# Gate and up of a routed feed-forward layer from operands split into two rounded parts, high and low parts of the rows side by side

## The reference

```python
C = max(1, math.ceil(T * K * CAP_FACTOR / E))        # 592 * 2 * 1.25 / 8 = 185 rows per expert
xb = buf[:E * C].reshape(E, C, D)                    # normalised rows, 8 x 185 x 256
gu = jnp.einsum('ecd,efd->ecf', xb, w12)             # 2048 columns: gate and up
g, u = jnp.split(gu, 2, axis=-1)
h = jax.nn.silu(g) * u
yb = jnp.einsum('ecf,edf->ecd', h, w3)
```

## Time and profile before

| | us |
|---|---|
| median of 3 runs | 254.06 |
| lowest, highest | 251.88, 254.31 |
| the profiled execution, its own time | 253.29 |
| its span, first to last instruction | 251.3 |
| mean granted TensorE clock | 0.892 of full |
| TensorE busy, matmuls | 206.7 (82%) |
| VectorE busy | 88.1 (35%) |
| ScalarE busy | 76.7 (31%) |
| POOL busy | 55.6 (22%) |

### The profile page before, as it was taken

How to read it: one execution, slowest core, us unless ns; L and a number is a source line. 1 busy time by engine, 2 the same in 40 slices (tenths; PEclk the granted TensorE clock), 3 DMA queues, 4 the chain that set the end, 5 groups by cost and what they waited for, 6 DMA issues and landing times.

```text
span 251.3 us, 3542 instructions
## 1 busy us (share of the span) xinstructions
PE 206.7 (82%) x1297; PEld 187.9 (75%) x1297; DVE 88.1 (35%) x277; ACT 76.7 (31%) x226; POOL 55.6 (22%) x55
## 2 busy tenths in 40 slices
PE   0185957989997774089999999999999999999970
PEld 0175947964765543079999999999999999999960
DVE  6849874444578745002211111111211112111110
ACT  2433311734544213011722222232222223322230
POOL 0445343000014445200002104003040040220404
PEclk9999995995589755558999999999999999999997
DMA  7935995510002122268109239077191480400101
GB/s 244 339 109 131 334 340 223 214 81 1 0 27 69 61 62 84 67 169 305 81 5 394 106 124 388 6 292 241 26 430 54 188 329 3 167 9 3 22 9 16
DMA packets 10299, 36.15 MB, mean 144 GB/s; under 512 B 3328, under 2 KB 6738, under 8 KB 7978
## 3 DMA queue, kind: packets, MB, share of 16 engines
q1 hardware_dynamic: 7514, 31.90, 35.0%
q0 software_dynamic: 2336, 2.13, 4.3%
q10 hardware_dynamic: 432, 1.90, 2.1%
HBM read 31.42 MB, written 5.35 MB: 146 GB/s over the span
## 4 chain that ended last, share of the span: by engine, by line
PE 71%; DVE 8%; DMA 7%; issue 5%; POOL 4%; ACT 2%; POOLq 1%; SPq 1%
PE bank L536 34%; PE bank L548 16%; DMA x_flat<-in 5%; PE bank L520 3%; DVE hn L765 2%; PE bank L467 2%; POOL token_rows L991 2%; PE bank L422 2%; PE bank L559 1%; POOL rstd L978 1%; PE bank L435 1%; PE bank L386 1%; PE bank L447 1%; PE bank L388 1%; PE bank L387 1%
## 5 line engine op out<-in xcount | busy, mean ns | idle before, releaser
L536 PE MATMUL bank<-xb,w 128*128 128x185 f32 x512 | 94.4, 329 | 1.1 <-ACT xb L687 1.1
L536 PEld LDWEIGHTS bank<-xb,w 128*128 128x128 f32 x512 | 84.8, 196 | 1.7 <-issue 1.2
L949 DVE TENSOR_TENSOR hid<-bank,sg 128x185 f32<-128x185 f32 x64 | 22.5, 351 | 116.8 <-ACT sg L699 116.8
L1008 POOL DMA_INDIRECT out<-yw,slot_token x16 | 23.8, 1489 | 122.1 <-ACT yw L719 119.7
L548 PE MATMUL bank<-hid,w 128*128 128x185 f32 x256 | 50.2, 320 | 0.0
L699 ACT ACTIVATE sg<-bank 128x185 f32<-128x185 f32 x64 | 20.9, 326 | 92.1 <-PE bank L536 92.1
L548 PEld LDWEIGHTS bank<-hid,w 128*128 128x128 f32 x256 | 42.1, 189 | 0.0
L335 PE MATMUL bank<-wp_hi,x_hi 128*111 128x256 f32 x36 | 11.2, 310 | 12.7 <-DVE x_lo L771 12.7
L335 PEld LDWEIGHTS bank<-wp_hi,x_hi 128*111 128x111 f32 x36 | 7.0, 194 | 12.9 <-issue 12.9
L991 POOL DMA_INDIRECT token_rows<-rowbuf,dest x12 | 11.6, 968 | 13.4 <-DVE dest L908 11.6
L520 PE MATMUL bank<-ident,rows_in 128*128 128x128 f32 (+1 forms) x32 | 7.9, 300 | 7.1 <-DMA rows_in<-token_rows 7.1
(11 more groups left out here) (137 smaller groups left out, 254.3 us busy)
## 6 DMA issues: line engine op xcount, KB each, us to landing
w<-in SPq DMA_DIRECT2D x8, 2048.0 KB, 10.7
w<-in SPq DMA_DIRECT2D x8, 1024.0 KB, 4.8
x_flat<-in SPq DMA_DIRECT2D x6, 333.0 KB, 10.8
token_rows<-rows_in SPq DMA_DIRECT2D x1, 1728.0 KB
rows_in<-token_rows SPq DMA_DIRECT2D x8, 144.0 KB
w_sb<-in ACTq DMA_DIRECT2D x1, 1024.0 KB, 9.0
wp_sb<-in ACTq DMA_DIRECT2D x1, 768.0 KB, 5.7
out<-h SPq DMA_DIRECT2D x5, 111.0 KB
```

What stands on the lines that cost most here:

```text
L536: mm = pe.matmul(o, w[:, part, k, :], xb[b][:, k, :], start=(k == 0), stop=(k == KD - 1))
L949: dve.tensor_tensor(hid[:, step % 4, :], bank[GU_BANK[step % len(GU_BANK)]][:, NS:2 * NS], sg[:, step % 2, :], ALU.mult).then_inc(hid_done, 1)
L1008: pool.indirect_dma_start(out=out, out_offset=bass.IndirectOffsetOnAxis(ap=slot_token[0:n, e, s:s + 1], axis=0), in_=yw[b][s][0:n, :], in_ ...
```

## The change

`gate_up` no longer multiplies float32 operands. The rows of an expert are first scaled to float32 (`xf`), then VectorE's new `split_tokens` copies them as fp32r (the high part) and subtracts that for the low part; both lie side by side in `xb`, 186 columns each (`NP`, 185 made even). The weights of each step go through a ring of 4 places (`w_ring`): ScalarE's `weight_hi` rounds 512 columns, VectorE's `weight_lo` subtracts. For each of 4 pairs of part and half TensorE now does a wide matmul, the high weights with all 372 columns, and a narrow one, the low weights with the 186 high columns, added to the first 186 columns of the result. Gate and up take one bank each, and two pairs of banks are used in turn. ScalarE copies the second halves of both banks out (`take_lo`), VectorE adds them to the first halves (`total`), and `silu` and `hidden` read the sum from SBUF. `gate_up` waits for `sum_done` of the step two earlier. SP waits for `w12_lo_done` where it waited for `gate_up_in_psum`, and `xf` is one buffer where `xb` was two and still is.

```diff
+NP = NS + NS % 2
+RING = 4
...
-        bank = [ctx.enter_context(nc.psum_tensor(f"bank{i}", [P, 512], F32)) for i in range(8)]
+        psum = ctx.enter_context(nc.psum_tensor("psum", [P, 8, 512], F32))
+        bank = [psum[:, i, :] for i in range(8)]
...
-        xb = [sb(f"xb{b}", [P, KD, NS]) for b in range(2)]
+        xf = sb("xf", [P, KD, NS])
+        xb = [sb(f"xb{b}", [P, KD, 2, NP], F32R) for b in range(2)]
+        w_ring = sb("w_ring", [P, RING, 2, PIECE], F32R)
         sg = sb("sg", [P, 2, NS])
+        gu = sb("gu", [P, 2, 2, NP])
+        gu_lo = sb("gu_lo", [P, 2, 2, NP])
         hid = sb("hid", [P, 4, NS])
...
                 if e >= 3:
-                    sp.wait_ge(gate_up_in_psum, FC * (e - 2))
+                    sp.wait_ge(w12_lo_done, FC * (e - 2))
                 sp.dma_start(w12[e % 3][:, :], w12T[e]).then_inc(w12_in[e % 3], 16)
...
-            GU_BANK, YT_BANK, XB_BANK, Y_BANK = (0, 1, 2, 7), (3, 4), 5, 6
+            GU_BANK, YT_BANK, XB_BANK, Y_BANK = ((0, 1), (2, 3)), (4, 7), 5, 6
...
                 pe.wait_ge(rows_back[e], 48)
                 if e >= 1:
-                    pe.wait_ge(xb_done, KD * e)
+                    pe.wait_ge(xf_done, KD * e)
...
             def gate_up(e, fc):
 
                 step, b = FC * e + fc, e % 2
+                pe.wait_ge(w12_lo_done, step + 1)
                 if fc == 0:
-                    pe.wait_ge(w12_in[e % 3], 16 * (e // 3) + 16)
-                    pe.wait_ge(xb_done, KD * (e + 1))
-                if step >= len(GU_BANK):
-                    pe.wait_ge(hid_done, step - len(GU_BANK) + 1)
-                w = w12[e % 3][:, fc * PIECE:(fc + 1) * PIECE].rearrange("p (n k f) -> p n k f", n=2, k=KD)
+                    pe.wait_ge(xb_done, e + 1)
+                if step >= 2:
+                    pe.wait_ge(sum_done, step - 1)
+                hi, lo = (w_ring[:, step % RING, n, :].rearrange("p (n k f) -> p n k f", n=2, k=KD) for n in range(2))
                 for part in range(2):
-                    o = bank[GU_BANK[step % len(GU_BANK)]][:, part * NS:(part + 1) * NS]
+                    o = bank[GU_BANK[step % 2][part]][:, 0:2 * NP]
                     for k in range(KD):
-                        mm = pe.matmul(o, w[:, part, k, :], xb[b][:, k, :], start=(k == 0), stop=(k == KD - 1))
+                        mm = pe.matmul(o, hi[:, part, k, :], xb[b][:, k, :, :].rearrange("p a c -> p (a c)"), start=(k == 0), stop=False,
+                                       skip_group_check=True)
+                        mm = pe.matmul(o[:, 0:NP], lo[:, part, k, :], xb[b][:, k, 0, :], start=False, stop=(k == KD - 1),
+                                       skip_group_check=True)
                 mm.then_inc(gate_up_in_psum, 1)
...
             def take_tokens(e):
                 act.wait_ge(xT_in_psum, e + 1)
+                if e >= 1:
+                    act.wait_ge(xb_done, e)
                 for k in range(KD):
-                    act.activation(xb[e % 2][:, k, :], bank[XB_BANK][:, k * D:k * D + NS], ACT.Identity,
-                                   scale=gamma_t[:, k:k + 1], bias=beta_t[:, k:k + 1]).then_inc(xb_done, 1)
+                    act.activation(xf[:, k, :], bank[XB_BANK][:, k * D:k * D + NS], ACT.Identity,
+                                   scale=gamma_t[:, k:k + 1], bias=beta_t[:, k:k + 1]).then_inc(xf_done, 1)
+
+            def take_lo(e, fc):
+                step = FC * e + fc
+                act.wait_ge(gate_up_in_psum, step + 1)
+                if step >= 2:
+                    act.wait_ge(sum_done, step - 1)
+                act.activation(gu_lo[:, step % 2, :, :], psum[:, 2 * (step % 2):2 * (step % 2) + 2, NP:2 * NP],
+                               ACT.Copy).then_inc(gu_lo_done, 1)
+
+            def weight_hi(step):
+                if step % FC == 0:
+                    act.wait_ge(w12_in[step // FC % 3], 16 * (step // FC // 3) + 16)
+                if step >= RING:
+                    act.wait_ge(gate_up_in_psum, step - RING + 1)
+                act.activation(w_ring[:, step % RING, 0, :], w12[step // FC % 3][:, step % FC * PIECE:(step % FC + 1) * PIECE],
+                               ACT.Copy).then_inc(w12_hi_done, 1)
 
...
             def silu(e, fc):
                 step = FC * e + fc
-                act.wait_ge(gate_up_in_psum, step + 1)
+                act.wait_ge(sum_done, step + 1)
                 if step >= 2:
                     act.wait_ge(hid_done, step - 1)
-                act.activation(sg[:, step % 2, :], bank[GU_BANK[step % len(GU_BANK)]][:, 0:NS], ACT.Silu).then_inc(silu_done, 1)
+                act.activation(sg[:, step % 2, :], gu[:, step % 2, 0, 0:NS], ACT.Silu).then_inc(silu_done, 1)
...
+            for step in range(RING - 1):
+                weight_hi(step)
             take_tokens(0)
             for e in range(EXPERTS):
                 for fc in range(FC):
+                    take_lo(e, fc)
+                    if FC * e + fc + RING - 1 < STEPS:
+                        weight_hi(FC * e + fc + RING - 1)
                     silu(e, fc)
...
-                dve.tensor_tensor(hid[:, step % 4, :], bank[GU_BANK[step % len(GU_BANK)]][:, NS:2 * NS], sg[:, step % 2, :],
+                dve.tensor_tensor(hid[:, step % 4, :], gu[:, step % 2, 1, 0:NS], sg[:, step % 2, :],
                                   ALU.mult).then_inc(hid_done, 1)
 
+            def weight_lo(step):
+                dve.wait_ge(w12_hi_done, step + 1)
+                dve.tensor_tensor(w_ring[:, step % RING, 1, :], w12[step // FC % 3][:, step % FC * PIECE:(step % FC + 1) * PIECE],
+                                  w_ring[:, step % RING, 0, :].bitcast(F32), ALU.subtract).then_inc(w12_lo_done, 1)
+
+            def total(e, fc):
+                step = FC * e + fc
+                dve.wait_ge(gu_lo_done, step + 1)
+                both = psum[:, 2 * (step % 2):2 * (step % 2) + 2, :]
+                dve.tensor_tensor(gu[:, step % 2, :, :], both[:, :, 0:NP], gu_lo[:, step % 2, :, :], ALU.add).then_inc(sum_done, 1)
+
+            def split_tokens(e):
+                dve.wait_ge(xf_done, KD * (e + 1))
+                if e >= 2:
+                    dve.wait_ge(gate_up_in_psum, FC * (e - 1))
+                dve.tensor_copy(xb[e % 2][:, :, 0, 0:NS], xf[:, :, :]).then_inc(xb_hi_done, 1)
+                dve.wait_ge(xb_hi_done, e + 1)
+                dve.tensor_tensor(xb[e % 2][:, :, 1, 0:NS], xf[:, :, :], xb[e % 2][:, :, 0, 0:NS].bitcast(F32),
+                                  ALU.subtract).then_inc(xb_done, 1)
+
+            for b in range(2):
+                dve.memset(xb[b][:, :, :, NS:NP].bitcast(F32), 0.0)
+            for step in range(RING - 1):
+                weight_lo(step)
+            split_tokens(0)
             for e in range(EXPERTS):
                 for fc in range(FC):
+                    total(e, fc)
+                    if FC * e + fc + RING - 1 < STEPS:
+                        weight_lo(FC * e + fc + RING - 1)
                     hidden(e, fc)
+                    if e + 1 < EXPERTS and fc == 6:
+                        split_tokens(e + 1)
```

More of the change, by code:

```diff
@@ L241, in vit_tower @@
         slots_done = sem("slots_done")
+        xf_done = sem("xf_done")
+        xb_hi_done = sem("xb_hi_done")
+        w12_hi_done = sem("w12_hi_done")
+        gu_lo_done = sem("gu_lo_done")
+        sum_done = sem("sum_done")
+        w12_lo_done = sem("w12_lo_done")
         gate_up_in_psum = sem("gate_up_in_psum")
```

4 lines of the change are left out of this document (2 added, 2 removed).

## The result

| | before | changed |
|---|---|---|
| median of the runs, us | 254.19 (4 runs) | 263.28 (4 runs) |
| lowest, highest | 251.88, 254.48 | 262.38, 265.43 |
| ratio, 95% interval | | 1.039 (1.030 to 1.049) |
| profiled execution, its span | 253.29, 251.3 | 264.17, 262.2 |
| mean granted clock | 0.892 | 0.872 |

The change makes the kernel 9.1 us slower, where 259.0, 4.8 over that median, was forecast. A second set of runs gave 263.75 against 254.23, ratio 1.048 (1.036 to 1.061). Medians are of all runs and ratios of each kernel's fast runs alone (those within 1.5% of its fastest), so a ratio need not be the quotient of two medians.

What follows compares the result with a forecast made beforehand. TensorE was taken to bound the expert loop. Matmuls -8.5 us, turn +7.8, `take_yT` +3.0, expert 0 +2.0, both ends +0.5 and +0.9 make +5.7 on 253.3: 259.0 us; own range 256 to 262, overall 248 to 269.

Steps and rivals of the forecast that it cites:

- the sum: All gains and losses of the prediction added up: 5.7 us slower than the profiled execution's 253.3.
- one event that had 5%: Rival at the first `gate_up`: the clock stays at 0.50 beyond 115.2 us, costing 3.0 us, 262 us in all; 5%.
- Matmuls: `gate_up` in each of 64 steps: pair 280 ns (wide 168, narrow 112), step 1.12 us for 1.25, 8.5 us less.
- both rivals on the narrow matmul: Narrow matmul in `gate_up`: 89 ns by columns alone, 254.6 us (15%); or not one pass, 268.0 or 300 us (17%).
- The turn: Turn to the next expert, 7 times: TensorE waits 1.1 us for the split rows, 7.8 us more.
- `take_yT`: Before `down(e, 0)`, 7 times: `take_yT` queued behind the SiLU of fc = 1 stalls TensorE 0.43 us, 3.0 us more.
- Expert 0: Table loads and exponential hold ScalarE: `gate_up` of fc = 7 waits 0.55, the turn 2.6 instead of 1.1; 2.0 us more.
- Both ends: First `gate_up` waits 0.95 us for the split, costing 0.5; the last `down` waits for the last product, costing 0.9.
- Transfers and queues: SP's waits, DMA and POOL's scatter in the loop: cost nothing unless a transfer takes 19 us.
- The columns case: Rival in `gate_up`: narrow matmul at 89 ns, 5.9 us more gained, stalls 1.3 us longer; +1.3, 254.6 us; 15%.
- the estimate behind it: The columns case by the Trainium skill's figures, pair of 157.5 and 80 ns: -2.3, 251.0 us.

Runs made afterwards that it cites:

- the two experiments on it: The changed kernel with the narrow matmul left out, 242.25 us; and with three narrow matmuls in place of a wide and a narrow one, 263.42 us.
- the two with 1.90: The changed kernel with the next expert's rows one step earlier, 254.31 us; and the same with `take_yT` also ahead of the SiLU of fc = 1, 250.43 us.

## Why the prediction was right in direction and short in size

Loops are the fair comparison: 143.8 us on average before (six traces), 150.2 after without the fall of the clock, 152.9 and 153.1 with it. That is 6.4 more, and 9.1 to 9.3; the sum said 5.7. The medians differ by 9.1 and 9.5. So in the traces with the fall the terms of the sum carry two thirds, and one event that had 5% the rest. How many of the runs without a trace had it is not known, and the one trace without it took 263.01 us all the same, since its loop started late, at 110.8.

- **Matmuls.** An ordinary step went from 1.885 to 1.753 us, 0.132 less, and 0.1325 was forecast; pair 284 ns for 280 (wide 173 for 168, narrow 112 for 112). Right, and the two experiments on it exclude both rivals on the narrow matmul.
- **The turn.** Mechanism and place right, undone by the rows one step early; 1.24 us for 1.1, or 1.19 with the shorter step behind it, 0.5 us over seven. The chain was priced right: TensorE starts 3.35 us after the end of `gate_up(e, 6)` in the records (147.37 to 150.72), where 3.33 was forecast. What was off is when TensorE would have been free, 2.11 and not 2.23: the last `down` before the next `gate_up` takes 0.53 us from its start to that of the `gate_up` (147.20 to 147.73 for the one before), not 0.63.
- **`take_yT`.** 0.45 us by removal, 0.43 forecast. The transposes of L575 behind it, which were to stay as they are, cost more: with the stall gone the step with them and the next one take 0.51 us over two ordinary steps (2.31 and 1.71), and 0.44 before the change (2.32 and 1.89). 0.5 us over seven, which the sum did not have.
- **Expert 0.** 1.72 us beyond an ordinary turn, for 2.0. The wait of 0.55 at `gate_up` of fc = 7 did not come, and the turn was 2.96 over an ordinary step, more than the 2.6.
- **Both ends.** The first `gate_up` came 1.0 us later in the loop (0.95), and part of it displaced low-clock work: expert 0 had 4.5 us at 1.2 GHz (112.3 to 116.8). At the end the profile shows 0.64 us of waiting ahead of the last `down`, counted from a modelled end; from the start of the last `gate_up` to the end of the span it is 12.74 us where it was 11.84, so 0.9 as forecast.
- **Transfers and queues.** Nothing in the loop waited for them; POOL is as busy as it was, 56.4 us for 55.6. ScalarE is busy 73% of an expert (12.48 of 17.14 us), where the forecast had 65%; its own 1.35 of 1.75 us would be 77%.
- **Slips of the prediction's own sums.** The columns case adds up to +1.1 and 254.4 us, not +1.3 and 254.6; the estimate behind it, with a pair of 157.5 and 80 ns, comes to -2.8 and 250.5 us by the same working, not -2.3 and 251.0. The base of 253.3 lies 0.9 under the median of four. None of these changes which case came.

**The step that failed** is the clock. The case had 5%, 3.0 us, and its place at the first `gate_up`: "TensorE starts a microsecond later and stops more in expert 0; the level of 0.50 then lasts beyond 115.2 us". That level ended at 116.8 and cost nothing more. What came was a new stretch: TensorE stood still for 2.6 us before expert 1, the longest stop in the loop, which the sum contained, and the clock went down with it (at 130.5 us, where TensorE starts again at 131.0), 6.8 us at half speed, 2.6 us lost. The prediction had priced this stop as idle time and nothing else. With it the sum is 5.7 + 2.6 = 8.3, and 0.5 at the turns, 0.5 for the transposes and 0.1 at `take_yT`, less 0.3 at expert 0, make 9.1. The clock at the start of the loop is not separated from chance here: expert 0 of the kernel before took 16.3 to 17.9 us in six traces.

What is shown is narrower than a cause. Removing the table loads removes the long stop, and the fall did not come (one trace, 3.6 us less in the medians); all six traces of before, without the stop, have none. Two of three traces of the changed kernel have one, and so has that of the wide matmuls alone, with the same stop. The third had the same stop of 2.62 us and kept the full clock. Six traces with a shorter stop there or none (1.90 us twice, 1.47, 0.94, 0.57, none) have no fall, one trace each; the two with 1.90 still have the table loads, so the loads by themselves do not bring it. All falls came with the longest stop, and that stop did not decide it; what else must come together stays open.

## What to carry to other kernels

When matmuls get faster by handing work to other engines, count the instructions between the last matmul and whatever only one later step needs, and follow every queue to the rare work behind the new instructions (the turn, the output, a table load): 64 steps gained 8.5 us here and 14 waits took 11.5 back, until two pieces of rare work were moved one place forward. Price a matmul with its own weight load, which seems to set the pace at 186 columns (112 ns, where the columns alone would give 89). A stop of TensorE of 2.6 us cost 2.6 more in clock in two traces of three, so such a stop can be dearer than it looks. And compare the part that a change touches, from trace to trace, when single executions of one kernel differ by 7 us elsewhere: the loops told these versions apart where the medians hardly did.
